# A row of softmax shifts by four small transfers, and a rearranged opening: a graph attention layer on one core

## What is computed

```
h  = relu(layernorm(x))                       # the sources
hs = layer_norm(h, ln1);  ht = layer_norm(h_target, ln1)
q  = (ht @ Wq + bq) / sqrt(32);  k = hs @ Wk + bk;  v = hs @ Wv + bv
logits = q . k per head;  logits = where(adj != 0, logits, -1e30)
probs  = softmax(logits);  ctx = probs @ v
ht = layer_norm(ht + ctx @ Wo + bo, ln2)
out = x + ht + gelu(ht @ W1) @ W2
```

## Time and profile before

| | |
|---|---|
| median of three runs | 723.34 us |
| the profiled execution | 727.01 us |
| its span, first to last instruction | 725.2 us |
| PE busy | 672.5 us (93%) |
| DVE busy | 591.6 us (82%) |
| POOL busy | 517.4 us (71%) |
| ACT busy | 451.7 us (62%) |

### The profile page before, as it was taken

How to read it: one execution, slowest core, us unless ns; L and a number is a source line. 1 busy time by engine, 2 the same in 40 slices (tenths; PEclk the granted TensorE clock), 3 DMA queues, 4 the chain that set the end, 5 groups by cost and what they waited for, 6 DMA issues and landing times.

```text
span 725.2 us, 20296 instructions
## 1 busy us (share of the span) xinstructions
PE 672.5 (93%) x8386; PEld 479.8 (66%) x8386; DVE 591.6 (82%) x974; ACT 451.7 (62%) x806; POOL 517.4 (71%) x494
## 2 busy tenths in 40 slices
PE   4968889899999999999999999999999899889998
PEld 4536567666677677667767776677677667556667
DVE  5947687999989997999999899989977987554651
ACT  4632446666677656877766586677666778836650
POOL 3720657979899996789999778899977777442430
PEclk9979998999999999999999999999999999989999
DMA  8373610211200111130000201103000000000001
GB/s 296 112 196 79 236 31 2 70 45 57 81 2 2 31 57 34 44 104 17 2 31 2 89 30 54 38 2 118 2 2 2 3 2 2 1 1 23 23 22 52
DMA packets 20796, 36.22 MB, mean 50 GB/s; under 512 B 2752, under 2 KB 13280, under 8 KB 20704
## 3 DMA queue, kind: packets, MB, share of 16 engines
q1 hardware_dynamic: 20704, 34.92, 15.6%
HBM read 26.49 MB, written 2.10 MB: 39 GB/s over the span
## 4 chain that ended last, share of the span: by engine, by line
PE 56%; DVE 30%; issue 8%; SPq 2%; ACT 2%; DMA 1%; DVEq 0%; ACTq 0%
PE score L442 24%; DVE early L1147 14%; PE early L442 14%; PE ctx L442 10%; PE aux L442 6%; DVE prob_lo L1155 6%; SPq L358 2%; DVE mask_nat L1135 1%; DVE st_x L1070 1%; DVE half_max L1147 1%; DVE q_stage L1173 1%; DMA node_i<-in_nodemask 1%; DVE st_l L1065 1%; DMA kT<-mask_nat 1%; DVE col_l L1193 0%
## 5 line engine op out<-in xcount | busy, mean ns | idle before, releaser
L1350 POOL TENSOR_TENSOR prob_lo<-prob 128x512 f16<-128x512 f32 x376 | 434.9, 1181 | 109.8 <-ACT prob L856 108.3
L856 ACT ACTIVATE prob<-score 128x512 f32<-128x512 f32 x512 | 304.8, 597 | 173.9 <-PE score L442 166.2
L442 PE MATMUL early<-kT,qT 96*128 96x512 f16 x512 | 193.3, 383 | 28.1 <-DVE half_max L1147 20.8
L442 PE MATMUL score<-nidentb,mask_nat 128*128 128x128 bf16 x2048 | 198.9, 220 | 2.6 <-ACT prob L856 1.4
L442 PE MATMUL score<-qT,kT 97*128 97x512 f16 x512 | 196.0, 383 | 0.0
L442 PEld LDWEIGHTS ctx<-v_sb,prob 128*128 128x128 bf16 x2048 | 160.0, 98 | 54.3 <-ACT raw L878 9.3
L442 PE MATMUL ctx<-v_sb,prob 128*128 128x65 f16 x2048 | 192.3, 193 | 0.6 <-POOL prob_lo L1350 0.5
L442 PE MATMUL ctx<-v_sb,prob_lo 128*128 128x65 f16 x2048 | 191.1, 193 | 0.0
L1147 DVE CUSTOM_DVE_ANT_0 early<-early,mask_nat,half_max 128x1024 f32<-128x1024 f32 x128 | 163.6, 1285 | 28.4 <-PE early L442 27.9
L1147 DVE CUSTOM_DVE_ANT_0 early<-early,mask_nat 128x1024 f32<-128x1024 f32 x128 | 156.8, 1229 | 25.6 <-PE early L442 23.7
L442 PEld LDWEIGHTS ctx<-v_sb,prob_lo 128*128 128x128 f16 x2048 | 143.4, 97 | 50.2 <-issue 4.8
(11 more groups left out here) (167 smaller groups left out, 609.1 us busy)
## 6 DMA issues: line engine op xcount, KB each, us to landing
adj_in<-in_adj SPq DMA_DIRECT2D x26, 512.0 KB, 3.8
qT<-q_stage SPq DMA_DIRECT2D x48, 64.0 KB, 2.0
kT<-mask_nat SPq DMA_DIRECT2D x48, 64.0 KB, 2.0
raw<-in_x SPq DMA_DIRECT2D x4, 512.0 KB, 5.1
tgt<-in_L_gnn_h_target SPq DMA_DIRECT2D x4, 512.0 KB, 8.4
prob<-in_adj SPq DMA_DIRECT2D x4, 512.0 KB, 8.4
nT<-in_L_gnn_W SPq DMA_DIRECT2D x2, 1024.0 KB, 7.5
mask_nat<-in_x SPq DMA_DIRECT2D x1, 2048.0 KB, 8.3
```

The costliest lines, as they stand in the source:

```text
L442: return nc.tensor.matmul(dst, w, m, start=start, stop=stop, **more)
L856: nc.scalar.activation(prob[:, n % SLOTS, :], score[n % 2][:, :], ACT.Exp).then_inc(exp_done, 1)
L1350: nc.gpsimd.tensor_tensor(prob_lo[:, n % SLOTS, :], prob[:, n % SLOTS, :], prob_hi(n % SLOTS), ALU.subtract).then_inc(lo_sem["pool"], 1)
```

## The change

The row of shifts no longer goes through TensorE. ScalarE negates the maxima, as before in step 6, into `shift[:, u % 2, :]`, four columns of 2-byte elements, and SP moves each column of 128 partitions to a quarter of the row in `qT` by a transfer of its own (`place_shifts`, four transfers). The first scores of a unit wait for these four. SP's order in the loop is now: loads of `adj` marked (r, 0), the row of the next unit, loads marked (r, 1), and in r = 4 the twelve query placings.

The first stage changes as well:
- the last four loads of `adj` block 0 and the last load of targets are issued before the first placing; head pairs 0 and 1 are placed in the opening, head pairs 2 and 3 (30 transfers) after the row of unit 0 and the loads of W1 and W2;
- the mean row comes from the sums of the normed features: VectorE sums each of the four blocks (`feature_sums`), TensorE multiplies the result with Wv (two products of 256 columns), ScalarE and VectorE split it (`mean_high`, `mean_low`); the 32 products, two copies and two GpSimd operations go;
- in unit 0 GpSimd takes all low parts.

And the feed-forward: gain and bias of the second norm are applied to the turned block by ScalarE (`normed_high`: one more pass for each half block, into `h_full`), and `up_bias`, its copy and the four scalings of w1 go. `turn_block(1)` comes after group 2 instead of 3, `block_high(1)` after gelu 4 instead of 7, `block_low(1)` after gelu_low 5 instead of 7.

```diff
--- before.py
+++ after.py
-SHIFT_STEP = 8
+SHIFT_AT = 6
-LOAD_AT = [0, 0, 0, 2, 2, 3, 4, 4]
+LOAD_AT = [(0, 0), (0, 0), (0, 1), (2, 0), (2, 1), (3, 0), (4, 0), (4, 1)]
-DVE_LO = [(2, 6, 10, 14)] * (UNITS - 2) + [tuple(range(1, STEPS, 2))] * 2
+DVE_LO = [()] + [(2, 6, 10, 14)] * (UNITS - 3) + [tuple(range(1, STEPS, 2))] * 2
...
+                def place_shifts(u):
+
+                    sp.wait_ge(shift_ready, u + 1)
+                    row = q_block(u // H)[SHIFT_ROW:SHIFT_ROW + 1, u % H, :]
+                    for t in range(TT):
+                        sp.dma_start(row[:, t * P:(t + 1) * P], shift[:, u % 2, t:t + 1]).then_inc(shift_in[u % 2], 16)
...
+                for i in range(TT, PAIRS):
+                    load_adj(0, i)
+                sp.dma_start(tgt[:, 3 * TT:4 * TT, :], rows(h_target, 3)).then_inc(tgt_in[3], 16)
 
                 staged(0)
                 place_q(0, range(1))
                 staged(1)
                 place_k(0, range(1))
-                for i in range(TT, PAIRS):
-                    load_adj(0, i)
-                place_q(0, range(1, TT))
+                place_q(0, range(1, 2))
                 staged(2)
                 place_k(1, range(1))
-                place_k(0, range(1, TT))
+                place_k(0, range(1, 2))
                 staged(3)
                 place_k(2, range(1))
+                place_k(1, range(1, 2))
                 staged(4)
                 place_k(3, range(1))
-                for c in range(1, NTB):
-                    place_k(c, range(1, TT))
-                sp.dma_start(tgt[:, 3 * TT:4 * TT, :], rows(h_target, 3)).then_inc(tgt_in[3], 16)
+                for c in (2, 3):
+                    place_k(c, range(1, 2))
 
                 sp.wait_ge(v_ready, NT // 2)
+                sp.wait_ge(feat_done, 1)
+                place_shifts(0)
                 for i, (dst, w) in enumerate(((w1, W1), (w2, W2))):
                     sp.dma_start(dst, w.rearrange("(c p) n -> p c n", p=P)).then_inc(w_in[i], 16)
+                for g in range(2, TT):
+                    place_q(0, range(g, g + 1))
+                    for c in range(NTB):
+                        place_k(c, range(g, g + 1))
                 for u in range(UNITS):
                     k, r = divmod(u, H)
                     if k + 1 < NTB:
                         for i in range(PAIRS):
-                            if LOAD_AT[i] == r:
+                            if LOAD_AT[i] == (r, 0):
+                                load_adj(k + 1, i)
+                    if u + 1 < UNITS:
+                        place_shifts(u + 1)
+                    if k + 1 < NTB:
+                        for i in range(PAIRS):
+                            if LOAD_AT[i] == (r, 1):
                                 load_adj(k + 1, i)
...
-                        pe.wait_ge(aux_done, AUX["shift", u] + 1)
+                        pe.wait_ge(shift_in[u % 2], TT * 16 * (u // 2 + 1))
...
-                def shift_row(u):
-                    pe.wait_ge(shift_ready, u + 1)
-                    aux_free(("shift", u))
-                    for t in range(TT):
-                        last = mm(aux[0:SHIFT_ROW + 1, t * P:(t + 1) * P], shift[:, t, :], ident16[:, :], True, True)
-                    last.then_inc(aux_ready, 1)
...
+                def mean_values():
+
+                    pe.wait_ge(feat_done, 1)
+                    pe.wait_ge(v_lo, NT // 2 - 1)
+                    for c in range(DC):
+                        last = mm(ctx[:, 0:D], feat_all[:, c:c + 1].to_broadcast([P, P]), wkv[:, 1, c, :], c == 0, c == DC - 1)
+                    last.then_inc(mean_ready, 1)
...
                 def negated(u):
                     act.wait_ge(max_done, (u + 1) * PAIRS)
-                    if u > 0:
-
-                        act.wait_ge(aux_ready, AUX["shift", u - 1] + 1)
-                    else:
-                        act.wait_ge(zeroed, 2)
-                    nc.scalar.activation(shift[:, :, SHIFT_ROW], half_max[:, u % 2, 1, :], ACT.Copy, scale=-1.0).then_inc(
-                        shift_ready, 1)
-
-                def row_out(u):
-                    job_here("shift", u)
-                    nc.scalar.activation(q_block(u // H)[SHIFT_ROW:SHIFT_ROW + 1, u % H, :], aux[SHIFT_ROW:SHIFT_ROW + 1, :],
-                                         ACT.Copy).then_inc(aux_done, 1)
+                    if u > 1:
+
+                        act.wait_ge(shift_in[u % 2], TT * 16 * (u // 2))
+                    nc.scalar.activation(shift[:, u % 2, :], half_max[:, u % 2, 1, :], ACT.Copy, scale=-1.0).then_inc(shift_ready, 1)
...
                 def normed_high(k, c, bank):
-                    nc.scalar.activation(h_bufs[k % 2][:, 0, c, :], bank, ACT.Copy).then_inc(h_hi, 1)
+                    if k > 0:
+
+                        act.wait_ge(h_lo, DC * (k - 1) + c + 1)
+                    else:
+                        act.wait_ge(w_lo, 4)
+                    read, count = (h_done, DC * (k - 1) + c + 1) if k > 0 else (aux_done, AUX["hT", 0, c] + 1)
+                    affine(h_full[:, c, :], bank, LN2_G[:, c:c + 1], LN2_B[:, c:c + 1]).then_inc(read, 1)
+                    act.wait_ge(read, count)
+                    nc.scalar.activation(h_bufs[k % 2][:, 0, c, :], h_full[:, c, :], ACT.Copy).then_inc(h_hi, 1)
...
                 for f in range(FC):
                     gelus(0, f)
+                    if f == 4:
+                        block_high(1)
                     if f in (5, 6):
                         context_T(NTB - 1, f - 5)
-                block_high(1)
...
+                def feature_sums(c):
+                    dve.wait_ge(nT_masked, DC * (c + 1))
+                    return nc.vector.tensor_reduce(feat_sum[:, :, c], nT[:, c, :, :], AX, ALU.add)
```

More of the change, by code:

```diff
@@ L107, in aux_numbers @@
 def aux_numbers():
-    jobs = [("mean", 0), ("mean", 1), ("shift", 0)] + [aux_job(u, s) for u in range(UNITS) for s in range(STEPS) if aux_job(u, s)]
+    jobs = [aux_job(u, s) for u in range(UNITS) for s in range(STEPS) if aux_job(u, s)]
     jobs += [("cT", NTB - 1, c) for c in range(DC)] + [("wo", NTB - 1, i) for i in range(TT // 2)]
@@ L266, in gnn_kernel @@
         adj_here = [sem(f"adj_here{i}") for i in range(PAIRS)]
-        q_first = sem("q_first")
-        k_first, k_placed, q_placed = [sem(f"k_first{i}") for i in range(NTB)], [sem(f"k_placed{i}") for i in range(NTB)], [sem(f"q_placed{i}") for i in range(NTB)]
+        k_placed, q_placed = [[sem(f"k_placed{c}_{g}") for g in range(TT)] for c in range(NTB)], [sem(f"q_placed{g}") for g in range(TT)]
         ones_placed = sem("ones_placed")
@@ L281, in gnn_kernel @@
         early_ready, max_done = sem("early_ready"), sem("max_done")
-        shift_ready = sem("shift_ready")
+        shift_ready, shift_in = sem("shift_ready"), [sem(f"shift_in{i}") for i in range(2)]
         score_ready, exp_done = sem("score_ready"), sem("exp_done")
@@ L334, in masks_free @@
                 for c in range(NTB):
-                    eng.wait_ge(k_first[c], FIRST)
-                    eng.wait_ge(k_placed[c], REST)
+                    for g in range(TT):
+                        eng.wait_ge(k_placed[c][g], PLACE)
             else:
@@ L363, in place_q @@
                         for r, part in enumerate((0, 1, 0)):
-                            place(q_block(k), q_stage, g, part, r, q_first if k == 0 and g == 0 else q_placed[k])
+                            place(q_block(k), q_stage, g, part, r, q_placed[g])
                 def place_k(c, groups):
@@ L630, in turn_normed @@
                     return last
-                def up_bias():
-                    pe.wait_ge(w_in[0], 16)
-                    aux_free(("bf", 0))
-                    for f in range(FC):
-                        for c in range(DC):
-                            last = mm(aux[:, f:f + 1], w1[:, c, f * P:(f + 1) * P], LN2_B[:, c:c + 1], c == 0, c == DC - 1)
-                    last.then_inc(aux_ready, 1)
                 pe.wait_ge(made, 3)
@@ L964, in _ @@
                     high_values(i)
-                act.wait_ge(q_first, FIRST)
-                act.wait_ge(q_placed[0], REST)
-                for g in range(2):
-                    mean_out(g)
+                mean_high()
                 negated(0)
-                row_out(0)
                 for n in range(AHEAD):
@@ L996, in _ @@
                             if (r, s - 2) in QP_AT:
-                                if k > 0 and QP_AT[r, s - 2] == 0:
-                                    act.wait_ge(q_placed[k], PLACE)
+                                if QP_AT[r, s - 2] == 0:
+                                    for g in range(TT):
+                                        act.wait_ge(q_placed[g], PLACE * (k + 1))
                                 query_high(k + 1, QP_AT[r, s - 2])
@@ L1020, in gelus @@
                         act.wait_ge(g_lo_done, j - 1)
-                    nc.scalar.activation(gelu[:, f % 2, :], up[f % 2][:, :], ACT.Gelu_apprx_tanh,
```

(10 more changed lines are left out.)

149 lines of the change are left out of this document (46 added, 103 removed).

## The result

The kernel after takes **898.08 us** (median of four runs, 896.44 to 900.58) against 723.35 for the kernel before on the same chip: a ratio of 1.2417, 95% interval 1.2388 to 1.2447. It is slower by 175 us. The forecast was 727.5, with a range of 711 to 740; the result lies far outside it.

The account below looks back on a forecast made before the run. TensorE was taken as the main bound, VectorE next. Gains of 3.6 us up to head 2 and 1.1 in the feed-forward against 8.9 lost at boundaries made +4.2: 731.2 profiled, 727.5 on the median, range 711 to 740.

Parts of the forecast that it names:

- I take 0.66 and 1.9: Row transfers: issues 0.66 us apart and a landing of 1.9, giving 4.2 us from negation to scores.
- the high end 6.2: Upper bound from negation to scores: issues every 0.69 us and a landing of 3.8, so 6.2 us.
- What bounds the kernel: Whole kernel: 56% of the chain on TensorE, 30% on VectorE; in the loop, full units keep TensorE busy throughout.
- The opening, -4.9: Up to the first scores: early products start at 43.0, first scores at 71.1 instead of 75.97, -4.9 us.
- Unit 0, +6.4: First unit: head 1's row queues behind 30 placings and loads, its scores start at 96.7 instead of 95.16, +6.4 us.
- Unit 1, -5.1: Second unit: without the up-bias, but with a late row and a half-clock restart, 18.1 instead of 23.16, -5.1 us.
- The boundaries, +8.9: The 30 boundaries behind unit 1: row 0.48 us later each in full units, other edits included, +8.9 us in all.
- The two other items: In the loop: w1 scalings leave VectorE, about -1.0 us; the transpose in unit 29 no longer waits, -1.2.
- The counts of the sum, 13, ten, seven and the last: Boundaries by kind: 13 full units +6.2 us, ten at half +2.4, three of seven +1.5 together, the last +1.0.
- The feed-forward, -1.1: Feed-forward: -3.9 us at block 1, +1.75 at block 2, +1.1 for a possible clock fall, so -1.1.
- The +1.75 for block 2: Feed-forward: block_high(2) stands on the path TensorE waits for; its longer ScalarE passes cost 1.75 us.
- Rival (b): Row transfers: two-byte writes are slow, each 0.9 us more of landing costs 22 in all, total 750; chance 0.12.

Follow-up runs that it names:

- e4: Kernel after with only the first of the four row transfers issued and waited for, the other three quarters of the row left at zero: 717.05 us.
- e3: Kernel after with the same four transfers, but each element written to a partition of its own and the row left at zero: 732.77 us.
- e6: Kernel after with each of the four transfers writing into a different single partition of an unused tile, the row left at zero: 769.52 us.
- e5: Kernel after with one transfer of 128 elements of 8 bytes in place of the four, the shift left out: 716.79 us.
- e1b: Kernel after with the row again by four products and a copy, a repeat on another chip: 711.69 us, ratio 0.9817 to the kernel before.
- e10: Kernel after with 64 redundant mask products ahead of the wait for the row at each of 31 boundaries: 835.2 us.
- e12: Kernel after with one transfer of 128 2-byte elements, placed 20 bytes apart in one partition of an unused tile, shift left out: 716.05 us.
- e9: Kernel after with the row by products and the feed-forward of before, but block 1 split early as in the change: 714.71 us, ratio 0.9872 to before.
- e14: Kernel after with one 8-byte-element transfer made whole: queries reordered in qT, 97-row products reading moving columns in steps of four: 801.28 us, ratio 1.1046 to before.
- e11: Kernel after with one 8-byte-element transfer made whole: early products take every fourth target, mask products write every fourth PSUM column: 799.46 us, ratio 1.1026 to before.

## Why the prediction was wrong

The step that failed is one term: "I take 0.66 and 1.9, as the source and the target are both on chip as in the placings." The 0.66 held (in the boundary shown the issues are 0.51 to 0.66 apart). The landing did not. The transfers weren't alike to the placings in the one respect that counts: 128 elements of 2 bytes into a single partition. One lands in 2.8 instead of 1.8 (e4 against e3), and of four the last lands 5.4 after its issue. Negation to scores is 7.5 where the sum had 4.2 and the high end 6.2, which was made of the landing of large loads from memory. The term failed twice over: a lone landing is 0.9 longer than the 1.9 taken, and the sum let the four landings overlap (three issues, then one landing), where the queueing-up adds another 2.5. Four transfers into four partitions do overlap (e6).

Point by point:
- **What bounds the kernel**: held. TensorE's stream sets the end, each late row counts whole. In e3, where the elements are spread, the landing is the one that was taken, and the profiled execution takes 732.77 (forecast 731.2). Term by term, against before: -4.1 up to head 0 (forecast -4.9), +8.1 in unit 0 (+6.4), -4.5 in unit 1 (-5.1), +8.1 in heads 2 to 31 (+8.9), -1.8 behind (-1.1). That the loop's +8.1 is so near is luck in part: a bare unit takes 15.05 us and not 15.4, and nine other boundaries wait 1.1 to 1.4.
- **The opening, -4.9**: the part ahead of the row held. The early products ran from 42.61, and the stretch from 43 to 49 has full clock. The feature sums take 1.17 each (1.15 taken; not the mask's rate):
```profile
45.79 2.34 DVE L1087 TENSOR_REDUCE feat_sum<-nT 128x2 f32<-128x1024 f32 x2
```
 The negation came at 67.78 all the same, where 66.9 was forecast: VectorE waits 2.5 us for ScalarE's part of the last two value products, for which the sum had 0.7. The row then took 7.7 instead of 4.2, so that by the first mask product 0.5 of the 4.9 was left. In e3 head 0 starts 4.1 earlier than before, in e5 6.9.
- **Unit 0, +6.4**: the mechanism held (30 placings, then two loads, then the row; the placings took 22.2 in place of 20.5). Head 1's mask product starts at 104.98 instead of 96.7, of which 6 are the landing: the four were issued from 95.07 on.
- **Unit 1, -5.1**: the up-bias went, but the late row and the clock came. 20.96 instead of 18.1; with the row by products 16.4.
- **The boundaries, +8.9**: measured +161 in heads 2 to 31. Against e1b (485.7) it is 164: by e10, 57 of them are the clock, and the remaining 107 are 3.7 a unit, which is the later row (7.8 against 3.9 from negation to the first product of 97 rows, e10 against e1b). The forecast had no half clock at the boundaries at all, and for waits as short as it had them that was right: e3, whose boundaries wait 1.4 at the most, has a mean clock of 1.00 from head 2 to head 31. e6, with a wait of 1.5 at most boundaries, has 0.98 there. The two other items held: the scalings and the transpose were put at -2.2, and e1b is 2.8 under before. (The counts of the sum, 13, ten, seven and the last, make 31 for 30 boundaries; that is worth 0.2 us.)
- **The feed-forward, -1.1**: neither shown nor refuted, as it hangs on the clock. From head 31 to the end before needs 118.1, e12 and e3 116.3, so -1.8, and e1b 120.8, so +2.7. In e12 block 1 starts 1.2 earlier than before, as forecast, in e1b only 0.3. The wait of 3.37 is gone, but a new one has come: the four passes on ScalarE hold up the copy of the last context, and TensorE waits 2.7 for that (1.2 in e9, with two passes). In e12 it goes on at the upper level, in e1b and here at half clock:
```profile
804.91 1.09 PE L594 MATMUL aux<-ident,q_stage 128*128 128x128 f32 x4 [2.66 <-ACT cT L862]
805.79 2.58 PE L454 MATMUL score<-nTq,w_f 128*128 128x512 f16 x6
```
 That the clock could fall in such a gap was in the sum; the gap stood elsewhere than forecast, and why it falls in one execution and not in another stays open. The +1.75 for block 2 can't be told apart either: from the start of block 1 to that of block 2 e12 takes 1.3 more than e9.
- **Rival (b)** named the cause, two-byte writes, and a sign of it, "if they land in 2.8 or more". Its price was wrong: it raised the landing of one transfer and let the four overlap. At 0.9 us it had 22 us; here the excess over 1.9 is 3.5 us (5.4), and the clock comes on top. Its slope of 22 us per 0.9 would give 86 for 3.5; in the 29 units alone the wait took 107 and the clock 57. A chance of 0.12 and a range up to 740 were both too little for a transfer of which no row of the trace showed the like.

The Trainium skill, DMA: Bandwidth & Descriptors, "Specifications", has transfers below 512 B read, modified and written. That can't be what makes the difference here: elements of 4 and 8 bytes are as far below it and land in 1.9. The estimate of 0.34 us a row that I drew from the section "Bandwidth" of the same page of the Trainium skill was about ten times too low (3.5 us over a landing of 1.9): the packets are short here too, none of them is seen after 414 us, but the landings are not.

## What to carry to other kernels

- Before turning a column into a row by DMA, count the elements that one partition receives and their size. Here 128 elements of 2 bytes took 2.8 us to land, 4.8 in the median when four such transfers stood in line, and 128 of 4 or 8 bytes 1.9. Where no row shows such a transfer, the range has to go to many times the nearest row, or a transfer of that form has to be measured first.
- A wait on the busiest engine costs more than its length: 3.7 us of wait a unit brought another 2.0 by the lower clock. Filling an unavoidable wait with redundant products gave 63 us back.
- A cheaper transfer that needs another order of elements moves its price to whoever reads that order.

## What the runs showed of the hardware

- Into one partition, 2-byte elements arrive some 11 to 12 ns apart when transfers queue up: the landings of unit 15 are 1.1 to 1.8 us apart, 1.5 on average for 128 elements. This is worked out from landings; no view shows the single writes. Side by side or 20 bytes apart is the same (2.8), in four partitions four transfers go in parallel (2.9 each), and 4-byte and 8-byte elements show none of it (1.9, against 1.8 for 2-byte ones in 128 partitions). Whether 4-byte elements would queue up too when four transfers stand in line was not tried.
- 97 x 512 products whose moving columns lie 8 bytes apart take 0.24 us more than their 0.38 (e14). The Trainium skill, Advanced Engine Details and Errata, "SBUF Cachelines", asks for two hits on each line of 16 bytes; columns 8 bytes apart have two, so by that rule they should be free. The measurement differs, and decides.
- Where the mask products write every fourth PSUM column, a step takes 0.21 us more (e11 against e5); by the starts of the products about 0.17 of it lies between the four mask products. The Trainium skill, Advanced Engine Details and Errata, "PSUM Cachelines", says that a pattern that isn't contiguous slows products down; these runs agree.
- The stationary operand with every fourth column (early products of e11 and e14) shows no such price: their loads take 0.14 and 0.11 us where contiguous ones take 0.10, and the products 382 ns on average in e11 and 399 in e14, against 383 before. What is left of e11's 0.21 a step, 0.04 us, is the most that it can cost there.
